# A transformer layer on one core: unused buffers ahead of matmul operands, two context loads moved forward, the last values' spreads split, 13 idle matmuls added

## What is computed

```python
def reference(x, ctx_1024, mask_1x1xSxS2_ik1, ...):
    ...
    x = x + _L0_xattn_ref(_layernorm(x, axis=-1), ctx_1024, ctx_1024, mask_1x1xSxS2_ik1, ...)
    x = x + _L0_attn_ref(_layernorm(x, axis=-1), L0_attn_W_Q, L0_attn_W_K, L0_attn_W_V, L0_attn_W_O)
    x = x + _L0_ffn_ref(_layernorm(x, axis=-1), L0_ffn_router_w, L0_ffn_w0_kernel, ...)
    return x
```

## Time and profile before

| | |
|---|---|
| median of three runs | 516.66 us (516.65 to 517.7) |
| the profiled execution's own time | 520.1 us |
| its span, first to last instruction | 518.3 us |
| mean granted TensorE clock | 0.977 |
| TensorE busy | 486.1 us, 94% |
| VectorE busy | 391.1 us, 75% |
| ScalarE busy | 323.0 us, 62% |
| GpSimd busy | 271.7 us, 52% |

### The profile page before, as it was taken

How to read it: one execution, slowest core, us unless ns; L and a number is a source line. 1 busy time by engine, 2 the same in 40 slices (tenths; PEclk the granted TensorE clock), 3 DMA queues, 4 the chain that set the end, 5 groups by cost and what they waited for, 6 DMA issues and landing times.

```text
span 518.3 us, 18402 instructions
## 1 busy us (share of the span) xinstructions
PE 486.1 (94%) x6699; PEld 455.4 (88%) x6699; DVE 391.1 (75%) x987; ACT 323.0 (62%) x838; POOL 271.7 (52%) x362
## 2 busy tenths in 40 slices
PE   1898999899899999999998689999999999999997
PEld 1777889889889898998987679999999999999996
DVE  2544546476677768777679988999989999999984
ACT  1456776576667767776782356666667666666651
POOL 4125443445245464444544364998666666667660
PEclk9978999899899999999999997999999999999999
DMA  6614121111111111010005400556655646456302
GB/s 178 196 49 120 23 44 44 25 44 43 24 44 21 41 41 41 21 41 21 4 4 170 159 2 1 179 163 230 188 171 173 189 139 205 133 194 204 123 1 82
DMA packets 58126, 48.92 MB, mean 94 GB/s; under 512 B 20942, under 2 KB 49744, under 8 KB 58064
## 3 DMA queue, kind: packets, MB, share of 16 engines
q1 hardware_dynamic: 58064, 48.09, 31.7%
HBM read 46.86 MB, written 1.08 MB: 92 GB/s over the span
## 4 chain that ended last, share of the span: by engine, by line
PE 82%; DVE 5%; issue 4%; ACT 4%; DMA 4%; SPq 1%; DVEq 0%; POOL 0%; ACTq 0%; POOLq 0%
PE bank L226 20%; PE bank L228 19%; PE bank L227 19%; PE bank L647 4%; PE bank L669 3%; PE bank L615 3%; PE bank L572 3%; DMA ctx_raw<-in_ctx 2%; ACT Pr L1158 1%; DMA w_raw<-in_L_xattn_Wk 1%; PE bank L1054 1%; PE bank L933 1%; PE bank L805 1%; PE bank L765 1%; PE bank L537 1%
## 5 line engine op out<-in xcount | busy, mean ns | idle before, releaser
L226 PE MATMUL bank<-XT_lo,W_hi 128*128 128x256 f32 (+1 forms) x352 | 99.3, 282 | 0.3 <-DVE XT_lo L1934 0.3
L227 PE MATMUL bank<-XT_hi,W_lo 128*128 128x256 f32 (+1 forms) x352 | 99.0, 281 | 0.0
L228 PE MATMUL bank<-XT_hi,W_hi 128*128 128x256 f32 (+1 forms) x352 | 98.8, 281 | 0.0
L2337 POOL TENSOR_TENSOR W_lo<-raw,W_hi 128x256 fp32r<-128x256 f32 (+1 forms) x88 | 84.3, 958 | 7.0
L2219 POOL TENSOR_TENSOR Pr<-Pr,rinv 128x1028 f32<-128x1028 f32 (+2 forms) x32 | 60.4, 1889 | 49.2 <-DVE rinv L1514 48.5
L1158 ACT ACTIVATE Pr<-Sc,nmax 128x257 f32<-128x257 f32 x128 | 64.5, 505 | 29.3 <-DVE nmax L1503 24.8
L1974 DVE TENSOR_TENSOR W_lo<-raw,W_hi 128x512 fp32r<-128x512 f32 (+1 forms) x88 | 71.8, 817 | 4.9 <-ACT W_hi L1335 1.2
L2335 POOL CAST W_hi<-raw 128x256 fp32r<-128x256 f32 (+1 forms) x88 | 43.5, 494 | 53.4 <-PE bank L228 32.8
L1503 DVE CUSTOM_DVE_ANT_0 Sc<-bank,mask_add 128x257 f32<-128x257 f32 x128 | 47.0, 422 | 31.0 <-PE bank L615 17.4
L2146 DVE TENSOR_TENSOR hid_lo<-hid,hid_hi 128x256 fp32r<-128x256 f32 (+1 forms) x88 | 68.7, 781 | 1.5 <-ACT hid_hi L1410 1.5
L226 PEld LDWEIGHTS bank<-XT_lo,W_hi 128*128 128x128 f32 (+1 forms) x352 | 65.4, 186 | 0.4 <-issue 0.4
(11 more groups left out here) (248 smaller groups left out, 1342.8 us busy)
## 6 DMA issues: line engine op xcount, KB each, us to landing
raw<-in_L_ffn_w_kernel SPq DMA_DIRECT2D x32, 512.0 KB, 4.6
ctx_raw<-in_ctx SPq DMA_DIRECT2D x32, 256.0 KB, 2.8
raw<-in_L_ffn_wo_kernel SPq DMA_DIRECT2D x16, 512.0 KB, 5.7
raw<-in_L_ffn_w_kernel SPq DMA_DIRECT2D x16, 344.0 KB
last_prob<-Pr SPq DMA_DIRECT2D x128, 1.0 KB, 1.8
raw<-in_L_ffn_wo_kernel SPq DMA_DIRECT2D x8, 256.0 KB
x_sb<-in_x SPq DMA_DIRECT2D x4, 256.0 KB, 5.5
VL_all<-vl_rows SPq DMA_DIRECT2D x8, 128.0 KB
```

Source lines behind the costliest of these rows:

```text
L226: pe.matmul(dst, a_hi, b_lo, start=first, stop=False)
L227: pe.matmul(dst, a_lo, b_hi, start=False, stop=False)
L228: return pe.matmul(dst, a_hi, b_hi, start=False, stop=last)
L2337: po.tensor_tensor(W2_lo[0:w, m % RW, :], raw2[0:w, t, :], f(W2_hi[0:w, m % RW, :]), ALU.subtract)\
```

## The change

**Buffers.** Six tiles that no instruction uses are put into the allocation: 96 bytes a partition ahead of `ctxT_hi`, 32 ahead of `nmax`, 64 each ahead of `yT_hi`, `O2T_hi`, `W01_hi` and `hid_hi`. What is allocated behind them in the same scope moves by their sum. In the built programs the tiles of the split products begin at these remainders of the address by 128 bytes, hi and lo alike:

| tile | its partner | partner at | before | after |
|---|---|---|---|---|
| ctxT (keys, values) | WT | 0 | 96 | 64 |
| OT | WT | 0 | 64 | 64 |
| yT | WT | 0 | 0 | 64 |
| O2T | WT | 0 | 64 | 64 |
| W01 | XT | 32 | 32 | 96 |
| W2 | hid | 32 | 32 | 96 |

**Transfers.** The loads of contexts five and six go ahead of `vl_rows`; those of seven and eight (with the statistics of contexts one and two ahead of them) stand between the spreads, which go three, two and three.

**Idle products.** `idle` moves up and takes a bank's address; eight go ahead of the waits of "kl", five ahead of the wait after "vl". All idle products now use the first weight instead of the last.

```diff
+    sb("apart_ctxT", [P, 24], scope=early)
     ctxT_hi = sb("ctxT_hi", [P, 2, KH, 2 * P], F32R, early)
...
+    sb("apart_OT", [P, 8], scope=early)
     nmax = sb("nmax", [P, 2, G], scope=early)
...
+    sb("apart_yT", [P, 16], scope=early)
     yT_hi, yT_lo = sb("yT_hi", [P, KH, P], F32R, early), sb("yT_lo", [P, KH, P], F32R, early)
...
+    sb("apart_O2T", [P, 16], scope=early)
     O2T_hi, O2T_lo = sb("O2T_hi", [P, KH, P], F32R, early), sb("O2T_lo", [P, KH, P], F32R, early)
...
+    sb("apart_W01", [P, 16])
     W01_hi, W01_lo = sb("W01_hi", [P, RW, 2, KH, P], F32R), sb("W01_lo", [P, RW, 2, KH, P], F32R)
...
+    sb("apart_hid", [P, 16])
     hid_hi, hid_lo = sb("hid_hi", [P, RW, SL], F32R), sb("hid_lo", [P, RW, SL], F32R)
...
-        def load_ctx(j):
-            for u in range(4):
+        def load_ctx(j, first=0, end=4):
+            for u in range(first, end):
...
+        load_ctx(1, 0, 2)
         sp.wait_ge(sm["first_act"], slot("vl", 0) + 1)
         sp.dma_start(vl_rows, vl[:, :]).then_inc(sm["vl_out"], 16)
         sp.wait_ge(sm["vl_out"], 16)
-        for j in range(TT):
-            src = vl_rows[BT * j:BT * j + BT, :].unsqueeze(1).broadcast_to([BT, S, D])
-            sp.dma_start(VL_all[:, j, :], src).then_inc(sm["vl_in"], 16)
-        load_ctx(1)
+
+        def spread_last(tiles):
+            for j in tiles:
+                src = vl_rows[BT * j:BT * j + BT, :].unsqueeze(1).broadcast_to([BT, S, D])
+                sp.dma_start(VL_all[:, j, :], src).then_inc(sm["vl_in"], 16)
+
+        spread_last(range(0, 3))
+        load_ctx(1, 2, 3)
+        spread_last(range(3, 5))
+        load_ctx(1, 3, 4)
+        spread_last(range(5, TT))
...
+        def idle(n, at):
+
+            for _ in range(n):
+                pe.matmul(at[:, 0:D], WT_hi[:, 0, 0, 0:P], WT_hi[:, 0, 0, :], start=True, stop=True)
...
             elif kind == "kl":
+                idle(8, dst)
                 pe.wait_ge(sm["first_act"], n)
...
         prepare(slot("vl", 0))
+        idle(5, bk[7])
         pe.wait_ge(sm["first_act"], NS)
...
-        def idle(n, at):
-
-            for _ in range(n):
-                pe.matmul(bk[at][:, 0:D], WT_hi[:, 7, 0, 0:P], WT_hi[:, 7, 0, :], start=True, stop=True)
...
-        idle(8, 7)
+        idle(8, bk[7])
...
```

More of the change, by code:

```diff
@@ L971, in _ @@
         pe.wait_ge(sm["a_sum"], TT)
-        idle(8, 7)
+        idle(8, bk[7])
         turn_norm(z)
-        idle(6, 7)
+        idle(6, bk[7])
         project_self(z, False)
@@ L978, in _ @@
         pe.wait_ge(sm["r_neg"], 1)
-        idle(5, 5)
+        idle(5, bk[5])
         turn_qk(z)
-        idle(9, 5)
+        idle(9, bk[5])
         scores(z)
@@ L987, in _ @@
         pe.wait_ge(sm["b_v"], TT)
-        idle(3, 7)
+        idle(3, bk[7])
         turn_self_probs(z)
@@ L991, in _ @@
         dispatch(1)
-        idle(5, 7)
+        idle(5, bk[7])
         self_outputs(z)
         turn_router(y_)
-        idle(3, 7)
+        idle(3, bk[7])
         project_out(z)
@@ L1009, in _ @@
         dispatch(y_)
-        idle(4, 7)
+        idle(4, bk[7])
         dispatch(z)
-        idle(6, 7)
+        idle(6, bk[7])
         pe.wait_ge(sm["r_x_kept"], TT)
```

## The result

The changed kernel takes 511.09 us (median of four runs, 510.14 to 512.06; the profiled one 512.06, with a span of 510.3), beside 517.18 for the kernel before: 6.1 us less, ratio 0.9878 with a 95% interval from 0.9845 to 0.9910. The forecast was 501.8, a gain of 14.9, with a range of 498.0 to 509.5. Two executions were slow as a whole and stand outside the ratios: 1148.54 us of the kernel before (beside e1 to e4) and 515.86 us of e5.

The account below looks back on a forecast made before the run. The prediction took TensorE's own stream as the bound. Gains of 1.6 (idle products), 3.0 (early contexts) and 10.3 us (buffers), 14.9 in all, taken from 516.66 gave 501.8 us, with a range from 498 to 509.5.

Parts of the forecast that it names:

- What bounds the kernel: Whole kernel: TensorE is busy 486.1 of 518.3 us, 50.00 of 50 in the experts; only shortening its stream gains time there.
- Rival (b): Experts: VectorE takes over as the bound, so their 7.3 us are not had: 509.1 us; chance 0.10.
- Term 2: Early attention: loading contexts five and six early removes a 1.84 us wait and the low clock behind it: 3.0 us gained.
- Rival (c): Early attention: the statistics still land late and the gain from early contexts is 0: 504.8 us; chance 0.08.
- Term 1: Early contexts, 27 to 34 us: 13 idle products keep the clock up; 1.6 us gained, ends 2.3 gained and 1.2 lost.
- cost nothing: Early waits for QT and vl: at the full clock both sets of idle products hide in waits for ScalarE that stay.
- Term 3: Experts and attention: moved start addresses bring products closer, 0.1135 us apart at 64 bytes: 10.3 us gained, ends 0 and 12.
- Rival (a): Experts and attention: the buffers do nothing, only the clock and transfer gains count: 512.1 us; chance 0.12.
- (d): Early contexts: the idle products don't hold the clock and cost up to 1.2 us: 504.6 us; chance 0.05.
- (e): All moved tiles: slower, the new addresses as much worse as they were held better: 523.7 us; chance 0.03.
- The sum: Whole kernel: 1.6 + 3.0 + 10.3 = 14.9 us gained, from 516.66 to 501.8 us.

Follow-up runs that it names:

- e1: The kernel before with only the six unused buffers added: 512.24 us, ratio 0.9916.
- e4: The kernel before with only the 13 idle products added: 519.96 us, ratio 1.0050.
- e5: The changed kernel with one more unused 64-byte buffer ahead of W2, putting W2 at 32 and hid at 96: 508.45 us, ratio 0.9833.
- e3: The kernel before with only the early contexts and the spreads in three parts: 514.26 us, ratio 0.9945.
- g4: The changed kernel without the transfers, with 64 tiny transposes ahead that move TensorE's code by 128 instructions: 508.11 us.
- g1: The changed kernel, all three parts, with 64 tiny transposes ahead that move TensorE's code by 128 instructions: 503.07 us.
- g2: The changed kernel without idle products, with 77 tiny transposes ahead so that later code stands at the same place as in g1: 505.99 us.
- g5: The kernel before, none of the three parts, with 77 tiny transposes ahead so that later code stands as in g1: 512.76 us.
- g3: The changed kernel without the six buffers, with 64 tiny transposes ahead that move TensorE's code by 128 instructions: 508.72 us.
- f1: The changed kernel with the experts' moving tiles at 32 and stationary ones at 96, modulo 256 bytes: 508.23 us, ratio 0.9813.
- g6: f1 with 64 tiny transposes ahead that move TensorE's code by 128 instructions: 499.54 us, ratio 0.9667.
- e2: The changed kernel without the six buffers: 514.89 us, ratio 0.9967.
- e7: e3 with 26 empty TensorE instructions (looks at a semaphore) right behind its first wait: 517.31 us, ratio 0.9988.
- f2: The changed kernel with 230 TensorE instructions (looks at a semaphore) ahead, 256 with those of the idle products: 523.79 us, ratio 1.0123.

## Why the prediction was wrong, step by step

**What bounds the kernel.** Right: TensorE's stream alone counts, and VectorE with 45.86 of 50 us did not take over. Rival (b) is refuted.

**Term 2, contexts five and six early (3.0).** Right: 3.2 alone (e3), no wait for the load, none for the statistics, none for the spreads. Rival (c) is refuted. With the idle products present it is more, 5.0 (g4), since without it their gain goes into the wait for context five (2.71 us there). What the term did not see is that the statistics come late again further on, at 102.59 us of the changed kernel (a wait of 3.32 us on ScalarE, and of 2.19 us on TensorE behind it); in g1 ScalarE's waits for them between 60 and 262 us are 0.9 us.

**Term 1, the idle products (1.6).** Right on what it looked at: the clock holds, and both sets end at the waits that stay. At a fixed place of the code they are worth 2.9 (g2) (the far end of the term was 2.3, and the play covers the difference). In the change as made they are worth nothing: 510.43 without them, 511.09 with. The step that failed is "cost nothing": the sum priced 13 products by their time and not by their 26 instructions, which move all of TensorE's later code. Measured against the place 128 instructions further on, the code costs 8.0 us where the change put it, and 4.3 where it was. The prediction's rows for this were in the trace, three waits by "issue" of 0.6 to 1.7 us, and it did not read them. Terms 1 and 2 together, at one place, are 4.0 (g5 to g3; 4.8 by the ratios) where 4.6 was forecast. Taken away one at a time at that place, the three parts are worth 2.9, 5.7 and 5.0, 13.6 in all, and taken away together 9.7 (g5 to g1): they overlap.

**Term 3, the buffers (10.3).** This is the mis-sized term: 5.7 at one place of the code (g3 to g1), 5.2 alone (e1). In the profiles of g3 and g1 the experts give 3.3 (186.2 to 182.9 us) instead of 7.3, attention from the first to the last energies 1.9 (226.9 to 225.0) instead of 3.0. The failing step is the one that counted 0.1135 for every product at 64 apart from one short run of five products: at that offset there are two distances, and the prediction saw one of them. The trace of the kernel before had the other as well: OT stands at 64 too, and none of its eight runs is flat at 113 (at 108.56 us its gaps are 117, 118, 117, 119 and 117 ns), and one of O2T's eight is not. In the changed kernel, for the same 64 bytes, 20 of 27 groups of keys from 55 us on went below 115 ns and 26 of 27 groups of values stayed near 118; in g1 13 and 24 of 27 did. Rival (a), "no row shows one tile at two addresses", was the right doubt in the wrong measure: the addresses do act, by half. That 511.1 lies close to its 512.1 is chance: 5.7 us of the buffers were gained and 3.6 lost to the code. Rivals (d), in the way it was meant, and (e) are refuted.

**The sum.** 14.9, less 4.6 for the buffers, less 0.6 for the two first terms, less 3.6 for the code (9.7 between g5 and g1, 6.1 between before and after): 6.1, as measured. It closes because every step is a difference of the same medians; it proves no part by itself. The range failed because every end of it was an end of one of the three terms; nothing in it stood for what the change does to code that it doesn't touch.

What stays open: why one of the two borders flips the distance and the other keeps it, and why single groups still fall to 117.7 in e5, f1 and g6. Of attention's loss in the changed kernel, 3.8 and 0.6 us are stalls and 2.9 waits for VectorE, of which 2.19 stand behind ScalarE and the statistics. They are absent in g1, but e2 and e4, with stalls at the same products, have 0.5 us of them and none, so that what makes the statistics late is open.

## What to carry to other kernels

A rate read from one short run of products is a rate of that run: look for the same offset elsewhere in the trace (here OT), at nanoseconds and group by group, before multiplying by two thousand. Price added instructions by their place too: list the "issue" waits of the bounding engine before and after, and if they moved by the number of instructions added, try empty work in an idle stretch ahead to move them on. A gain in one part is then best measured with the code's place held.

## What was not expected of the hardware

One product form, 128x256 at the full clock with every other engine idle, had distances from 113.3 to 120 ns by its operands' addresses modulo 256, and two stable ones, 113.3 and 117.8, at one offset. TensorE stood for 0.2 to 2.0 us by "issue" in or close behind small products, at places that 26 instructions more moved and 256 restored (e7, f2), followed in some profiles by a fall of the granted clock to 0.50 (e7, and the kernel before); a shift of 26 instructions cost 2 to 3 us (e3 to e7), one of 128 saved 8 (the changed kernel to g1). An instruction that only looked at a semaphore took TensorE 0.11 us.
